# A transformer layer in full precision: where a piece of the score maxima, or the sums, stand among the scores of a slot

## The reference

```python
mod = jax.nn.silu(condition) @ Wada + bada
sh_a, sc_a, gt_a, sh_m, sc_m, gt_m = jnp.split(mod, 6, axis=1)
xn = _layernorm(x, g1, be1)
xm = xn * (1.0 + sc_a[:, None, :]) + sh_a[:, None, :]
x = x + gt_a[:, None, :] * _attention(xm, Wqkv, Wproj, bproj)   # causal, 16 heads
xn = _layernorm(x, g2, be2)
xm = xn * (1.0 + sc_m[:, None, :]) + sh_m[:, None, :]
h = jax.nn.gelu(xm @ W1 + b1, approximate=False)
x = x + gt_m[:, None, :] * (h @ W2 + b2)
```

## Time and profile before

| | |
|---|---|
| median of 3 runs | 3385.24 us (3382.95 to 3386.41) |
| the profiled execution's own time | 3385.02 us |
| its span in the trace | 3383.3 us |
| PE busy | 3211.6 us, 95% of the span |
| DVE, ACT, POOL busy | 61%, 35%, 46% |

### The profile page before, as it was taken

The page is one execution under the profiler, slowest core; times in us unless marked ns, Lnnn a source line. Parts: engine busy times, 40 slices in busy tenths (PEclk is TensorE's granted clock), DMA queues, the critical chain, the costliest instruction groups (busy, mean ns, idle before and its releaser), DMA issues.

```text
span 3383.3 us, 70508 instructions
## 1 busy us (share of the span) xinstructions
PE 3211.6 (95%) x25708; PEld 2581.8 (76%) x25708; DVE 2078.7 (61%) x2511; ACT 1167.8 (35%) x2322; POOL 1557.9 (46%) x1312
## 2 busy tenths in 40 slices
PE   7989999999999999988659999999999999999999
PEld 4656666766666667755458999999999989989898
DVE  5567777767777776676265555555555555555552
ACT  2245555555555555555411111111112112111111
POOL 2246566666666666677652323333223323333232
PEclk9999999999999999999879999999999999999999
DMA  5546565565656555666332223122221222222220
GB/s 213 189 129 185 174 180 171 169 176 167 177 178 184 164 172 175 174 174 169 102 94 74 54 59 74 53 59 68 60 59 60 62 64 53 62 71 53 59 62 13
DMA packets 303514, 391.88 MB, mean 116 GB/s; under 512 B 24240, under 2 KB 206000, under 8 KB 303336
## 3 DMA queue, kind: packets, MB, share of 16 engines
q1 hardware_dynamic: 289904, 367.84, 38.2%
q10 hardware_dynamic: 13440, 21.50, 1.8%
HBM read 270.66 MB, written 118.06 MB: 115 GB/s over the span
## 4 chain that ended last, share of the span: by engine, by line
PE 85%; DVE 9%; issue 3%; ACT 2%; DMA 1%; SPq 0%; DVEq 0%; ACTq 0%; POOL 0%
PE psH L858 22%; PE psY L871 21%; PE psA L677 10%; PE psT L718 7%; PE psA L755 6%; PE psP L837 5%; PE psA L673 4%; DVE mx L1162 4%; PE psS L693 4%; PE psA L728 3%; DVE psS L1158 2%; DVE xm_h L1136 1%; PE psA L646 1%; PE psP L847 1%; PE psT L620 1%
## 5 line engine op out<-in xcount | busy, mean ns | idle before, releaser
L1409 POOL TENSOR_TENSOR h_l<-h_full,h_h 128x256 fp32r<-128x256 f32 x512 | 489.7, 957 | 1120.1 <-DVE h_h L1329 1120.1
L940 ACT ACTIVATE e<-psT 128x512 f32<-128x512 f32 (+1 forms) x1202 | 605.2, 554 | 595.7 <-PE psT L718 593.8
L1449 POOL TENSOR_TENSOR es<-e 128x1024 f32<-128x1024 f32 (+1 forms) x320 | 624.0, 1950 | 392.4 <-PE psA L728 218.5
L1162 DVE TENSOR_REDUCE mx<-psS 128x4 f32<-128x2048 f32 (+3 forms) x384 | 666.1, 1756 | 214.3 <-PE psS L693 207.2
L1037 ACT ACTIVATE h_full<-psH,b1c 128x256 f32<-128x256 f32 x512 | 244.0, 477 | 1332.2 <-PE psH L858 1332.2
L858 PE MATMUL psH<-a_h,w1p_h 128*128 128x256 f32 x2048 | 577.9, 282 | 7.5 <-DVE a_l L1324 7.5
L858 PE MATMUL psH<-a_h,w1p_l 128*128 128x256 f32 x2048 | 580.3, 283 | 0.0
L858 PE MATMUL psH<-a_l,w1p_h 128*128 128x256 f32 x2048 | 579.9, 283 | 0.0
L1329 DVE CAST h_h<-h_full 128x256 fp32r<-128x256 f32 x512 | 148.3, 290 | 536.0 <-ACT h_full L1037 535.0
L718 PEld LDWEIGHTS psT<-qst,kst 97*128 97x128 f32 x2404 | 351.7, 190 | 120.1 <-issue 70.9
L718 PE MATMUL psT<-qst,kst 97*128 97x256 f32 (+1 forms) x2404 | 409.1, 290 | 13.3 <-ACT e L940 11.8
(11 more groups left out here) (113 smaller groups left out, 4762.4 us busy)
## 6 DMA issues: line engine op xcount, KB each, us to landing
qk_split<-qk_hl SPq DMA_DIRECT2D x128, 512.0 KB, 3.4
kst<-qk_split SPq DMA_DIRECT2D x128, 256.0 KB, 4.0
qst<-qk_split SPq DMA_DIRECT2D x128, 256.0 KB, 4.1
xin<-in_x_dram SPq DMA_DIRECT2D x64, 256.0 KB, 4.2
values<-vout ACTq DMA_DIRECT2D x64, 256.0 KB, 4.1
kmx<-qk_split SPq DMA_DIRECT2D x32, 512.0 KB, 4.7
qmx<-qk_split SPq DMA_DIRECT2D x32, 512.0 KB, 6.3
kst<-qk_split SPq DMA_DIRECT2D x128, 128.0 KB, 3.9
```

What stands on the lines that cost most here:

```text
L940: act.activation(e[:, s % ERING, 2 * hp:2 * hp + 2, 0:w], score_bank(s, hp, with_a)[:, :, 0:w], ACT.Exp, scale=SCALE).then_inc(sem("exp_do ...
L1162: reduce = dve.tensor_reduce(mx[:, part, :, qt], psS[:, :, col:col + w], AX_X, ALU.max)
L1409: return pool.tensor_tensor(dst, full, high.bitcast(F32), ALU.subtract)
L1449: pool.tensor_tensor(to, first, second, ALU.add).then_inc(sem("added"), 1)
```

## The change

It is in PE's queue alone, in the bodies without projection. Before, a slot's four half steps stood together, and then the piece (or the turn), the sums and the values. Now A and B stand first, then the piece if the slot has one, then C and D, then sums and values. In a slot without a piece, the sums stand between B and C. The turn at r = 13 also stands between B and C, ahead of the sums. A slot with neither stays as it was.

```diff
-                    for hp in range(2):
-                        scores(u, s, hp, with_a)
+                    if with_a:
+                        for hp in range(2):
+                            scores(u, s, hp, True)
...
                     if r == MAX_TURN_AT and not (last and h == 1):
                         max_turn(u, h + 1)
-                    if r in max_at(u, h):
-                        d, n = max_at(u, h)[r]
-                        if not (last and h + d >= 2):
-                            max_item(u, h + d, n)
+                    piece = max_at(u, h).get(r)
+                    if piece and last and h + piece[0] >= 2:
+                        piece = None
+                    if piece:
+                        max_item(u, h + piece[0], piece[1])
+                    t = s // 2
+                    sums = s % 2 == 1 and t >= 2 and (t - 2) % SLOTS not in DIAG_SLOTS
+                    between = not with_a and not piece
+                    if sums and between:
+                        added_sums(u, t - 2)
+                    if not with_a:
+                        for hp in range(2):
+                            scores(u, s, hp, False)
+                    if sums and not between:
+                        added_sums(u, t - 2)
                     if s % 2 == 1 and not (isinstance(u, int) and u == 0 and s == 1):
-                        t = s // 2
-                        if t >= 2 and (t - 2) % SLOTS not in DIAG_SLOTS:
-                            added_sums(u, t - 2)
                         values(u, t - 1)
```

## The result

The changed kernel is slower: 3396.98 us median (3390.28 to 3399.85) against 3385.84 (3382.19 to 3389.47), nine runs each, a ratio of 1.0029 with a 95% interval of 1.0019 to 1.0040. Forecast were 3375.4 us and a range up to 3380.3. The profiled execution took 3399.85 us, its span is 3398.1.

A forecast was written before the change was run, and what follows sets the result against it. PE was taken to set the pace in the free stretches, DVE in the chain; gains of 1.09 + 5.78 + 0.32 + 2.43 = 9.62 us off the profiled 3385.02 gave 3375.4 us, 8-in-10 range 3372.8 to 3380.3.

The forecast's parts named there:

- The chain: Piece 3 to the turn, at DVE's pace: 23.78 us before and after, PE's savings becoming longer waits for DVE.
- the first of the signs of being wrong: The forecast would be wrong if the stretch from piece 3 to the turn itself moved from 23.78 us.
- rival 3: Clock falls habitually at longer piece waits in the chain, 1.1 us each; 18 more give 3395.2 us; chance 0.05.
- the narrow pair: Two narrow score half steps moved behind the turn: 0.49 us, making turn to A of r = 15 2.14 instead of 1.65.
- first A of body 13 to piece 3: First slot of body 13: piece 3 at 1449.49, held by piece 2, instead of 1450.58; 1.09 us less.
- four free stretches: Turn to next item's piece 3, at PE's pace: 12.81 us against 14.14 or 14.37, together 5.78 less.
- rest of body 15's first item: Behind its turn: pair costs 0.49, r = 15 gives 0.34, r = 19 gives 0.47, r = 17 nothing; 0.32 us less.
- last item: Body 15's second item, no pieces: sums between pairs at six slots give 0.34 or 0.47 each, 2.43 us less.
- D's waits: PE's wait before D, 0.28 us at r = 15, vanishes: D comes about 1.45 after A, free at 1.25.
- The price of a change of kind: Step between kinds of matmul: 0.09 us added, so a wide pair takes 0.67, a narrow one 0.49.
- The copy-bound slots: Slots r = 1, 3, 11, 17: values wait for ACT's copy, 2.32 us after A at r = 17; no length gained.
- Rival 2: POOL's sum or masks, or ACT's copy, takes D's place as what PE waits for; 3380.5 us, chance 0.06.

The follow-up runs named there:

- experiment 1: Changed kernel, but at r = 11 C and D stand ahead of piece 8 again, as before; 3387.67 us, ratio 1.0000 to the kernel before.
- experiment 2: Changed kernel, with POOL's add of slot r = 11 made to wait for DVE's join in bodies without projection; 3382.64 us, ratio 0.9990.
- experiment 5: Changed kernel, with DVE's join written as two reductions that read one SBUF operand each; 3377.45 us, ratio 0.9975 to the kernel before.
- experiment 3: Changed kernel, with PE repeating 14 narrow score matmuls as filler while it would wait at the turn; 3386.90 us, ratio 0.9999.
- experiment 8: Changed kernel, but at r = 13 C and D stand ahead of the turn and the sums, as before; 3383.41 us, ratio 0.9991.
- experiment 10: Kernel before, with a one-operand join and 18 small spare DVE reductions ahead of it in the last five joins; 3397.86 us, ratio 1.0037.
- experiment 4: Kernel before, with POOL's add of slot r = 11 made to wait for DVE's join; 3392.24 us, ratio 1.0020.
- experiment 11: Changed kernel, with the order of before at r = 5 to 13 of the items with pieces, two-operand join kept; 3376.77 us, ratio 0.9972.

## Why the prediction was wrong

**The step that failed** is "*The chain.* Nothing: 23.78 before and after." The chain grew to 24.83 us, which was the first of the signs of being wrong that I had named. I had read the turn as DVE's pace ("and then comes the join"), with the join's 0.74 us as its own length. It was held by POOL's add, whose start hangs on C and D of r = 11, and these I moved behind piece 8 without asking who waits for their exponentials. I looked for PE waiting for POOL and found none; that DVE could be the one who waits, within an instruction's own duration, shows in no view of waits. Shown by experiments 1, 2 and 5.

**The clock** was rival 3, with a chance of 0.05, and looked for in the wrong place. It was the larger loss, and the sum had nothing for it. I looked for it at the waits for pieces, 0.9 us each. These brought one fall in the profiled execution, one fewer than before, and it cost the 1.1 us of my price (piece 6 to 7 again 4.75 us). The wait that does it is the one at the turn, which I never sized: it grew by 1.05 us from the late join, and because the narrow pair no longer filled it. That move I charged with 0.49 us behind the turn and nothing ahead of it. And a fall there costs more than my 1.1: 16.4 us for five, 3.3 each. They last longer, 37.4 us in all, and a microsecond at half clock costs 0.44 there, against 0.32 in the chain (1.1 for 3.4). I take the difference to be that behind the turn no wait for DVE takes part of the loss up; no run tests that. Shown by experiments 3, 8 and 10. The 3395.2 us of that rival lie near the measured 3396.98 by luck: they are 18 more falls of 1.1 us, none of which came.

**The account.** From body 13's first A to the last values the profiled executions differ by 239.14 - 224.81 = 14.33 us:

| term | forecast | measured |
|---|---|---|
| first A of body 13 to piece 3 | -1.09 | -1.10 |
| four free stretches, at full clock (13.14 in experiment 3) | -5.78 | -4.46 |
| rest of body 15's first item, at full clock | -0.32 | +0.30 |
| last item | -2.43 | -1.27 |
| join held longer, 5 x 1.05 | 0 | +5.25 |
| falls of the clock in the chain, 1.1 in place of 0.75 + 1.1 | 0 | -0.75 |
| half clock behind the turns: 14.82 in the free stretches, 1.54 in body 15 | 0 | +16.36 |

The medians differ by only 11.1, since the profiled execution was the slowest of the nine and how long the falls last varies.

**What was right, and what only mis-sized.** D's waits went away, and the sign of every term at full clock but one. The gains came to 6.5 us, not 9.6. The price of a change of kind was the term. Sums to C took 0.57 (1476.81 to 1477.38), where I had 0.45 for sums to values. A narrow pair took 0.59 to 0.60 in experiment 3, where I had 0.49; the 0.67 of a wide one was right. So the stretch from turn to A of r = 15 took 2.38 there instead of 2.14, and in the last item a wide slot gave 0.21 and a narrow one 0.23 instead of 0.34 and 0.47. The copy-bound slots (3.32 at r = 17) were right.

**Rival 2**, POOL in D's place, did not occur in the changed kernel; it did in experiments 2 and 4, where the add was delayed on purpose.

## What to carry to other kernels

Before moving work behind a step that waits, list who waits for that work on every engine, and not only in the semaphores: if a small DVE operation with two SBUF inputs lasts longer in one place than elsewhere, look whether it ends together with a POOL operation. And size the longest single wait of TensorE that a new order leaves, not the sum of its waits: here 24 waits of 1.0 us and less brought one fall of the clock, and a wait grown from 0.56 to 1.88 us brought one each time. Filling such a wait, even with useless matmuls, or shortening it, gave the loss back.

## What the runs showed of the hardware

- DVE's join of two SBUF operands beside POOL's add lasted until the add's end in all ten places looked at, 0.73 to 0.75 us before and 1.78 to 1.80 after, against 0.177 at the shortest; as a reduction of one SBUF operand it took 0.28 inside the same add, and a mask with one SBUF input and one in PSUM 0.70 inside an add as anywhere else.
- Behind waits of 1.77 to 1.89 us at the turn the granted clock fell to half in ten of ten places (the changed kernel and experiment 10), behind 1.75 to 1.78 in two of five (experiment 1), behind 0.29 to 0.94 in none of twenty (experiments 2, 3, 5, 8), and in experiment 11 behind none of four waits of 0.54 to 0.56 but behind one of 0.81. So the length of the wait alone does not decide, and what decides between the cases near 1.77 stays open. A fall lasted 3.4 to 10.2 us.
- The five falls in the changed kernel cost 16.4 us in the profiled execution, more than the whole gain of the change.
